# Three bank pairs and values by halves in the first maxima of two long cross attentions

## What is computed

```python
q = (jnp.einsum('bld,ed->ble', x, Wq) + bq).reshape(b, l, h, dh)
kv = (jnp.einsum('bmc,ec->bme', y, Wkv) + bkv).reshape(b, m, h, 2 * dh)
k, v = (kv[..., :dh], kv[..., dh:])
scale = 1.0 / jnp.sqrt(jnp.asarray(dh, x.dtype))
att = jax.nn.softmax(jnp.einsum('blhd,bmhd->blmh', q, k) * scale, axis=2)
out = jnp.einsum('blmh,bmhd->blhd', att, v).reshape(b, l, d)
return jnp.einsum('bld,ed->ble', out, Wo) + bo
```

## Time and profile before

| | us |
|---|---|
| median of 3 runs | 662.75 |
| the runs | 660.69 to 663.55 |
| the profiled execution, its own time | 660.76 |
| its span | 658.9 |

### The profile page before, as it was taken

One profiled execution on the slowest core, in us unless ns is written; L12 is line 12 of the kernel. 1 busy time (PEld: TensorE's weight loads), 2 busy tenths in 40 slices (PEclk: granted clock), 3 DMA queues, 4 the chain that ended last, 5 costly groups with the idle time before them and its releaser, 6 DMA issues. The chain is left out here.

```text
span 658.9 us, 12012 instructions
## 1 busy us (share of the span) xinstructions
PE 510.0 (77%) x4818; PEld 324.5 (49%) x4819; DVE 437.2 (66%) x851; ACT 300.7 (46%) x369; POOL 133.3 (20%) x199
## 2 busy tenths in 40 slices
PE   8989996788789996438994593772578488999756
PEld 4645663575255564313442263472556335556545
DVE  5764326746968955744999999925546596785243
ACT  2868882325566684111754560020112164768511
POOL 2211100000000000205698999300000000000000
PEclk9999997989999998556997688795569679999959
DMA  8544490753200000001022035051300150000000
GB/s 212 140 125 133 118 357 9 225 129 87 88 2 2 2 2 3 1 0 50 0 85 111 0 147 128 1 129 42 127 1 1 36 252 1 2 2 2 2 0 3
DMA packets 17258, 45.46 MB, mean 69 GB/s; under 512 B 4153, under 2 KB 13226, under 8 KB 16362
## 3 DMA queue, kind: packets, MB, share of 16 engines
q1 hardware_dynamic: 17076, 44.47, 22.4%
q0 software_dynamic: 128, 0.23, 0.1%
HBM read 34.28 MB, written 8.29 MB: 65 GB/s over the span
## 5 line engine op out<-in xcount | busy, mean ns | idle before, releaser
L251 POOL TENSOR_TENSOR rstd<-rstd,minus_half 64x1 f32<-64x1 f32 x20 | 11.8, 589 | 421.7 <-DVE rstd L259 421.7
L1531 ACT ACTIVATE ring<-psum,l3x_gain_columns 128x1024 f32<-128x1024 f32 x49 | 54.4, 1114 | 22.9 <-PE psum L1423 22.9
L1531 ACT ACTIVATE ring<-psum,l1x_gain_columns 128x1024 f32<-128x1024 f32 x49 | 54.4, 1114 | 22.4 <-PE psum L1423 22.4
L1437 PE MATMUL psum<-ring,values 128*32 128x128 f32 x1568 | 62.7, 279 | 0.4 <-ACT ring L1531 0.4
L944 ACT ACTIVATE ring<-psum,l0x_key_scale 128x1024 f32<-128x1024 f32 x49 | 52.4, 1114 | 9.9 <-PE psum L833 9.3
L1437 PEld LDWEIGHTS psum<-ring,values 128*32 128x32 f32 x1568 | 36.9, 109 | 28.1 <-issue 24.7
L1636 DVE TENSOR_REDUCE l3x_tops<-psum 128x1 f32<-128x448 f32 x64 | 36.7, 620 | 10.2 <-PE psum L1412 10.1
L1636 DVE TENSOR_REDUCE l1x_tops<-psum 128x1 f32<-128x448 f32 x64 | 36.7, 619 | 10.2 <-PE psum L1412 10.1
L3220 DVE MAX8 l2x_best<-values 128x8 f32<-128x6272 f32 x6 | 40.1, 6692 | 0.1
L3228 DVE MATCH_REPLACE8 values<-l2x_best,values 128x6272 f32<-128x6272 f32 x6 | 40.1, 6676 | 0.0
L1423 PE MATMUL psum<-l3x_Q_stack,wide 98*128 98x256 f16 x196 | 29.7, 275 | 2.1 <-DVE l3x_Q_stack L1595 1.3
(11 more groups left out here) (782 smaller groups left out, 1084.4 us busy)
## 6 DMA issues: line engine op xcount, KB each, us to landing
wide<-keys_aside SPq DMA_DIRECT2D x54, 224.0 KB, 3.7
experts<-in_experts SPq DMA_DIRECT2D x1, 4608.0 KB, 13.4
experts<-in_experts SPq DMA_DIRECT2D x1, 4096.0 KB, 15.8
keys_aside<-ring SPq DMA_DIRECT2D x7, 448.0 KB, 2.4
keys_aside<-experts SPq DMA_DIRECT2D x6, 448.0 KB, 2.6
ring<-in_ctx_tiles SPq DMA_DIRECT2D x1, 2352.0 KB, 9.7
experts<-in_experts SPq DMA_DIRECT2D x1, 2048.0 KB, 7.8
ctx_t<-in_ctx_t SPq DMA_DIRECT2D x3, 672.0 KB, 8.0
```

Source lines behind the costliest of these rows:

```text
L1437: last = nc.tensor.matmul(ps[32 * quarter:32 * quarter + 32, O_BANK, 128 * half:128 * half + 128], mem.values[:, at:at + 32], probs[:, t % ...
L1531: nc.scalar.activation(probs[:, t % PROBS, :].rearrange("p (b n) -> p b n", b=2), ps[:, pair:pair + 2, :], ACT.Exp, scale=exp_gain[:, :]). ...
```

## The change

The stage of both long attentions is changed in its part before the first exponentials, and little behind it.

- The first maxima use three bank pairs in turn (0-1, 2-3, 4-5), for both query halves. A pair of products waits until the pair three before it has been read.
- Only the first late super of values is projected ahead of the scores. The others (three in l1x, none in l3x) are projected by half supers of 4 and 3 tiles (`project_half`), one behind each second pair, into banks 6 and 7 by turns. ACT copies them by halves (`copy_half`), two behind the score copies of a half super.
- Products that nobody reads (`beside_maxima`, bank 7) follow the pairs: one behind the first of two, two behind the second; in l1x from n = 4, in l3x from n = 1.
- `Q_stack` is announced in two halves, and the products of a pair wait only for theirs. ACT makes its `Q_stack` copies before the values copy, DVE makes its own before the last two low parts of the keys.
- The second half of the top rows of chunk 0 is written by ACT instead of DVE (`first_top`).
- The copies of `Q_stack` for chunks 1 and 2 and the residual move behind the top of chunk 0.

The diff, cut to its core:

```diff
-    SLOTS = (5, 6, 7)
+    SLOTS, VALUE_BANKS = (5, 6, 7), (6, 7)
...
+    halves_of_values = [(n, half) for n in late_values[1:] for half in range(2)]
+    ALL_VALUES = 1 + len(halves_of_values)
+    UNREAD_FROM = (len(halves_of_values) + 1) // 2 + 1
+
+    def half_tiles(n, half):
+        return range(n * TPS + 4 * half, n * TPS + (TPS if half else 4))
...
+    pairs = [(n, s, p) for n, s in first for p in range(2)]
+
+    def pair_bank(n, s, p):
+
+        return 2 * (pairs.index((n, s, p)) % 3)
...
+                def project_half(i):
+
+                    n, half = halves_of_values[i]
+                    pe.wait_ge(values_copied, max(1, i))
+                    for at, t in enumerate(half_tiles(n, half)):
+                        last = nc.tensor.matmul(ps[:, VALUE_BANKS[half], at * C:(at + 1) * C],
+                                                mem.ctx_t[0:CTX + 1, t * 128:(t + 1) * 128], mem.w(pack, "Wv"),
                                                 start=True, stop=True)
                     last.then_inc(values_projected, 1)
...
-                for n in late_values:
-                    project("V", n)
-                pe.wait_ge(*act_done.at("Q_stack"))
-                pe.wait_ge(*dve_done.at("Q_stack"))
+                project("V", late_values[0])
                 if late_keys:
                     pe.wait_ge(low_ready, len(late_keys))
-                pe.wait_ge(values_copied, len(late_values))
-
-                for n, s in first:
-                    u, half = n // 2, slice((n % 2) * HALF, (n % 2 + 1) * HALF)
+
+                def beside_maxima(count):
+
+                    for _ in range(count):
+                        nc.tensor.matmul(ps[:, SLOTS[-1], 0:HALF], Q_stack[0:96, 0, 0, 0:128], stack[0:96, 0, 0, 0:HALF],
+                                         start=True, stop=True)
+
+                for n, s, p in pairs:
+                    u, half, at = n // 2, slice((n % 2) * HALF, (n % 2 + 1) * HALF), pairs.index((n, s, p))
                     pe.wait_ge(*stacked_with(u))
-                    for g in range(G):
-                        if n >= 1 and g % 2 == 0:
-                            pe.wait_ge(*first_read(n - 1, s, g // 2))
...
+                    pe.wait_ge(*act_done.at(f"Q_stack{p}"))
+                    pe.wait_ge(*dve_done.at(f"Q_stack{p}"))
+                    if at >= 3:
+                        pe.wait_ge(*first_read(*pairs[at - 3]))
...
+                    if p == 1 and 2 * n + s < len(halves_of_values):
+                        project_half(2 * n + s)
+                    if n >= UNREAD_FROM:
+                        if (n, s, p) == (UNREAD_FROM, 0, 0):
+                            pe.wait_ge(values_copied, ALL_VALUES)
+                        beside_maxima(1 + p)
...
-                pe.wait_ge(*first_read(first[-1][0], 0, 0))
+                pe.wait_ge(*first_read(*[pair for pair in pairs if pair_bank(*pair) == 0][-1]))
                 keep_on(14)
...
+                    for i in range(2 * n, min(2 * n + 2, len(halves_of_values))):
+                        copy_half(i)
+                act.wait_ge(top_turned, 2)
+                nc.scalar.activation(Q_stack[96:98, 0, :, :].rearrange("p g n -> p (g n)")[:, 512:1024],
+                                     ps[96:98, SLOTS[1], :], ACT.Identity).then_inc(*act_done.mark("first_top"))
...
                 raise_top(0)
+                dve.wait_ge(*act_done.at("Q_stack1"))
+                dve.wait_ge(*dve_done.at("Q_stack1"))
+                for k in range(1, N_CHUNKS):
+                    v.tensor_copy(Q_stack[0:96, k, :, :], Q_stack[0:96, 0, :, :])
+                step(v.tensor_tensor(residual[:, :], mem.x[:, :], mem.row(f"{pack}_bo"), ALU.add))
```

74 lines of the change are left out of this document (43 added, 31 removed).

## The result

| | before | after |
|---|---|---|
| median of the runs, us | 661.77 | 670.09 |
| the runs | 660.69 to 663.55 (4) | 667.31 to 672.45 (4) |
| span of the profiled execution | 658.9 | 667.2 |
| mean granted clock | 0.863 | 0.849 |
| PE busy, us | 510.0 | 526.1 |

The ratio of after to before is 1.0109, with an interval of 1.0071 to 1.0147: slower by 7.2 us, or by 8.3 us by the medians. Nine later runs of the same kernel beside 24 of the kernel before gave 669.28 against 663.12, a ratio of 1.0077 (1.0044 to 1.0110). Ratios leave out the runs that took over 1.5% longer than the fastest of their kernel, while medians, lowest runs and profiles take in all. The forecast was 663.3, which is 6.8 us too low.

What follows compares the result with a forecast made beforehand. Both stages were taken as bound by DVE once started, and before that by what lets it start. l1x +2.7 and l3x -2.1 gave +0.6 us on the profiled execution, so 662.75 becomes 663.3 us, range 659.3 to 666.3.

Steps and rivals of the forecast that it cites:

- Rounds, +0.5 at the folds' end without the clock: l1x first maxima: six rounds take 21.6 us, so DVE's folds end at 179.1 instead of 178.59, +0.5 us.
- The ring through ACT: l1x rounds: each half projection waits for an earlier half copy queued behind ACT's score copies; 4.1 us a round, twice.
- Clock ahead of the first scores, +1.8: l1x start: PE's 2.6 us idle gap brings a clock fall, about 4 us at half speed, +1.8 us.
- Rival 3: l1x: low clock stays over the halves for two rounds, costing 5.2 instead of 1.8 us; 668.3 us, chance 0.10.
- The later `keep_on`, +0.3: l1x behind the maxima: PE's 29 products start about 1.0 us later, done at folds' end + 3.4, +0.3 us.
- The top rows and the load, +0.1: l1x: ACT's top rows gain 0.4, but the exposed table load puts the first exponential at turning + 2.6, +0.1 us.
- rival 4: l1x: table load holds ACT longer as the engine empties around it, 1.3 us more; 664.6 us, chance 0.07.
- l3x, -2.1: l3x: earlier start and rounds -2.0, slow clock +0.2, later keep_on +0.1, top rows -0.4; sum -2.1 us.
- Unread products hold the clock: Rounds of both long attentions: products nobody reads keep PE working, so the clock stays up; they fit at full clock.
- rival 5: Last rounds: unread products fail to hold the clock, following products run at 0.37, about 1 us more; 664.3 us, chance 0.05.
- The stages that the diff leaves alone, 0: Stages outside l1x and l3x: the diff touches nothing else, so all terms come from those two and none from here.
- the prediction's own sign of being wrong: Stages behind the long attentions: the prediction called itself wrong if they change by more than 1 us.

## Why the prediction was wrong

The forecast added up to +0.6 us on the profiled execution; +8.3 was measured. Of the 7.7 us between them, 3.0 lie in the first tiles of l1x, 5.8 in stages that the sum held to be unchanged (2.9 ahead of l1x, 2.7 between, 0.2 behind), and 0.5 in the rest of l1x behind the ninth exponential; the start of l1x lost 0.8 less than forecast and l3x gained 0.5 more. Term by term:

- *First reduction, 3.8 us earlier:* right. 3.75 in the profile of after, 3.91 with the clock at full speed.
- *Rounds, +0.5 at the folds' end without the clock:* nearly. The ring through ACT is there, as are its waits; at the full clock the folds end 0.14 earlier than before, so up to there they took 21.1 us and not 21.6.
- *Clock ahead of the first scores, +1.8:* the size is right for the fall that was forecast (31.63 against 29.98, 1.7 us), but not what it was set against. The sum read in one execution that a gap of 1.55 us had no fall behind it. In three of the five profiles of the old l1x the clock fell behind this gap, each time for 6.8 us; behind the gap of 2.4 us of the new one, where it had been full before, it fell in two of six, for 3.4 us. And the half speed right behind l1x, which the sum put down to a gap of 2.44 us, had begun 0.7 us into that gap, at 259.5. In the four other profiles without a fill there the clock was half from the keys on, 1.1 or 1.2 us behind the stage's start: for 6.8 us in one, and for 13.7 us, to the second round, in three, which costs 3.0. Rival 3 had such a long stretch, but behind the gap, and at 5.2 us; these began 8 us ahead of the first scores, in instructions that both kernels share. No profile shows that the start of the changed l1x loses more to the clock than that of the old one.
- *The later `keep_on`, +0.3:* right. Turning starts 3.37 us behind the folds' end, forecast 3.4.
- *The top rows and the load, +0.1:* **this is the step that failed within l1x.** Its instructions are right to 0.05 us, and rival 4 is refuted: 0.02 us lie between the end of the load and the exponential. But the step priced only what lies on ACT, and the sum had nothing for the clock behind it: PE's wait for the first exponential grew from 0.86 to 1.39 us, and the first tiles then ran at half speed, at 3.0 us. In the first tiles of l1x the clock fell in all five profiles with the load exposed and no fill behind the top rows (four times for 6.8 us, which costs 3.0, once for 3.4), in two of the five with it hidden or early (both with the early load, 3.4 us, 1.5), in none of the five with a fill, and in none of the five with the old l1x. By the medians, taking the load away brings 7.8 us back, filling PE's waits 5.1, and putting 1.2 us of copies in the load's place takes 5.9 again. So that the exposed load and PE's waits belong to the fall is shown for these executions; that the length of the wait decides is not. The old l1x waits as long in sum (2.13 us) without a fall, the copies' 1.23 us had none in their profile, and twice 0.86 us had one. Nor is this step the whole loss: with DVE's casts the load is hidden again, and 4.5 us stay.
- *Moved copies, 0:* right. DVE is idle 2.75 us behind them.
- *l3x, -2.1:* right for the profile (-2.6), too good as a typical value. The clock rises between 7 and 14 us from the stage's start; where it rises at 9, the folds end at 26.5, where at 13.7, at 28.1 to 28.4, and the stage gains 0.8 to 1.1 instead of 2.6 where nothing else in it slows it. By the medians l3x alone gives about 1 us, less than its interval.
- *Unread products hold the clock:* right, and worth more than rival 5 had it: without them 6 us are lost, not 1.
- *The stages that the diff leaves alone, 0:* **this term failed too**, and by more. The sum said that all terms come from the changed stages. Those between them took 2.7 and 2.9 us more in the two profiles of the changed kernel, by the clock alone; that is the prediction's own sign of being wrong. The 2.9 us ahead of l1x in the first profile are an execution's and not the change's.

Rival 3 was the nearest in sign and size (668.3), but by luck: in the profile of after the stretch at the start of l1x is 3.4 us long and not over 7, and the loss lies elsewhere. What is shown is that the kernel is slower, that the change in l1x goes with it, and that the clock of TensorE is low where time is lost. How much each place is worth in the median stays open.

## What to carry to other kernels

Where an instruction is moved onto an engine's path, ask what TensorE does meanwhile, and do not price only its own duration: here 0.5 us of waiting moved to another place, and half speed over the next 7 us went with it. Products that nobody reads are worth trying in such waits, and so is a tiny activation that asks for a table load early; each took the changed kernel back to the time of the one before. Where the clock's low stretches stand at other places in each execution, one profile of before and one of after do not price a change: cut several of them by stage, take several of the kernel before too, and compare the untouched stages first.
